# Expert tiles of 256 rows, weights as the stationary operand, brought by DMA into one of two stages

## The chip, the cores and the metric

The kernel runs on one core of a Trainium2 chip. The metric is the device time of one execution in microseconds. The core has five engines with queues of their own: PE (matmul, with PEld for its weight loads), DVE, ACT, POOL and SP, which here issues plain DMAs; POOL issues the indirect ones.

## The reference, cut to what matters

One transformer layer on 4 x 1024 tokens of width 128: a gated linear attention over the sequence, then a mixture of experts. The change touches the routed part of the second:

```python
shared = sum(_ffn(xf, sw1[i], sw2[i], sw3[i]) for i in range(2))      # two experts for all tokens
logits = xf @ router_w.T + expert_bias
rw, sel = jax.lax.top_k(logits, 2)                                     # two of eight experts a token
rw = softmax(rw)
out = sum over the 8 experts of combine[:, e] * _ffn(xf, w1[e], w2[e], w3[e])
_ffn(x, w1, w2, w3) = silu(x @ w1.T) * (x @ w3.T) @ w2.T               # 128 -> 256 -> 128
```

## The kernel before

All engines run hand-written programs with semaphores. First come eight blocks of 512 tokens: the attention of block i beside the shared experts and the routing of block i-1. For every token and each of its two experts, POOL writes the normalised row (129 words: 128 values and, last, the row's number in `y_dram`) with an indirect DMA into that expert's region of `h_dram`. When all blocks are through, `table_of_tiles` on DVE makes, from the counts per expert, two tables: `tile_row`, the first row of each tile in `h_dram`, and `tile_expert`, its expert. A region's last tile is filled up with rows of `pads`, and the number of tiles is fixed (NTILE): 72 tiles of 128 rows, whatever the counts.

Then the tile stage, in TURNS turns of U = 12 tiles. Tile j passes through:

- SP loads `tile_row[j]` into a register and issues the DMA of 128 rows into `rows[:, u]`, one of U places (u is the tile's number in the turn). It waits before that for `s_yrow[u]`, the scatter of the tile that had the place before.
- PE, `rows_T`: transposes the rows into a bank `at`. ACT (`hi`) and DVE (`lo`) split them into two float32r halves in `t_hi` and `t_lo`.
- PE, `first`: three matmuls of 512 columns with the rows' halves as the stationary operand and the expert's `w13_hi` and `w13_lo` (all experts lie in SBUF) as the moving one. Their address comes from a register; the registers of a turn are loaded together at its head.
- ACT (`silu_rows`), DVE (`gated`): G = silu(first half) * second half, with the rows as partitions.
- PE, `G_T`: two transposes of G, and DVE (`take_GT`) copies them to SBUF.
- PE, `second`: two f32 matmuls with `w_2`, into `ybank` or `obank`. ACT (`take_y`) copies y into `y_sb[:, u]`.
- POOL: a one-column product (`carrier`) and the indirect DMA that scatters the 128 rows of y into `y_dram` and counts `s_yrow[u]`.

In step u of a turn PE runs first(u), rows_T(u + AHEAD), G_T(u - BEHIND_T), second(u - BEHIND_D), with AHEAD, BEHIND_T, BEHIND_D = 2, 2, 3; the other engines' queues have orders that match. After the last scatter has landed, SP loads y from `y_dram`, ACT, DVE and POOL combine both experts' rows with the weights and the residual, and SP stores the output.

`S`, the state of the attention, is free in the tile stage; `rows`, `y_sb` and `t_silu` lie in it.

Of the kernel before, what the change touches and what calls it, by code (L numbers as in the profile page):

```python
# [78 lines left out]
U = 12  # L79
RING = 4  # L80
AHEAD, BEHIND_T, BEHIND_D = 2, 2, 3


def build(nc, x, cmod, attw, wg12, w13T, w2T, bias, consts, ids, tiles, pads, H, out):
# [11 lines left out]
    REG = NTOK + P  # L96
# [4 lines left out]
    assert NTILE % U == 0 and U % RING == 0 and NTILE >= 2 * NTOK // P + NEXP - 1 and TURNS >= 3  # L101

    h_dram = nc.dram_tensor("h_dram", [NEXP * REG + (NTILE - 2 * NTOK // P) * P, ROW], F32).ap()
    y_dram = nc.dram_tensor("y_dram", [2 * NTOK + pads.shape[0] * P, P], F32).ap()
# [5 lines left out]
    with ExitStack() as ctx:  # L110
# [7 lines left out]
        def parts(whole, *widths):  # L118
# [127 lines left out]
        tile_expert = sb("tile_expert", [1, NTILE + BEHIND_D], I32)  # L246


        rows, y_sb, t_silu = (a.rearrange("p (u n) -> p u n", n=n) for a, n in zip(
            parts(S[:, :, :].rearrange("p v n -> p (v n)"), U * ROW, U * P, 2 * HID), (ROW, P, HID)))  # L250
        t_G = upd[:, 0:2, :].rearrange("p a (r n) -> p (a r) n", n=HID)
        t_GT = qS[:, :, :].rearrange("p a (r n) -> p (a r) n", n=HID)
        t_hi, t_lo = (a[:, :].rearrange("p (r n) -> p r n", n=P) for a in (vT_hi, vT_lo))
# [95 lines left out]
        s_trow = [sem(f"s_trow{u}") for u in range(U)]  # L349
        s_yrow = [sem(f"s_yrow{u}") for u in range(U)]  # L350
# [6 lines left out]
        s_tGt = sem("s_tGt")  # L357
        s_tGT = sem("s_tGT")
# [51 lines left out]
        def _(sp):  # L410
# [14 lines left out]
            sp.dma_start(h_dram[NEXP * REG:, :].rearrange("(n p) w -> n p w", p=P),  # L425
# [3 lines left out]
            for e in range(NEXP):  # L429
                r = sp.value_load(pad_row[0:1, e:e + 1], min_val=e * REG, max_val=e * REG + NTOK)  # L430
                sp.dma_start(h_dram[bass.ds(r, P), :], pads[e, :, :]).then_inc(s_pad, 16)
# [11 lines left out]
            for u in range(U):  # L443
                sp.wait_ge(s_yrow[u], 16 * TURNS)
# [14 lines left out]
        def _(pe):  # L459
# [279 lines left out]
            w_hi = w13_hi[:, NSH:, :].rearrange("p e n -> p (e n)")  # L739
            w_lo = w13_lo[:, NSH:, :].rearrange("p e n -> p (e n)")  # L740
            w_2 = w2_sb[:, NSH:, :, :].rearrange("p e c n -> p (e c n)")
            experts = []

            def rows_T(q, u):
                j = q * U + u
                wait(pe, s_trow[u], 16 * q + 16)
                wait(pe, s_thi, j - 1)
                wait(pe, s_tlo, j - 1)
                pe.transpose(at[u % 2][:, 0:P], rows[:, u, 0:P], ident[:, :]).then_inc(s_tr, 1)  # L749

            def first(q, u):
                j = q * U + u
                e = experts[BEHIND_D + u]
                wait(pe, s_thi, j + 1)
                wait(pe, s_tlo, j + 1)
                wait(pe, s_tG, j - 1)
                w = bass.ds(e * 2 * HID, 2 * HID)
                pe.matmul(ff[u % 2][:, :], t_lo[:, u % RING, :], w_hi[:, w], start=True, stop=False)  # L758
                pe.matmul(ff[u % 2][:, :], t_hi[:, u % RING, :], w_hi[:, w], start=False, stop=False)  # L759
                pe.matmul(ff[u % 2][:, :], t_hi[:, u % RING, :], w_lo[:, w], start=False, stop=True).then_inc(s_tf1, 1)  # L760

            def G_T(q, u):
                j = q * U + u
                wait(pe, s_tG, j + 1)
                wait(pe, s_tGT, j - 1)
                for c in range(NC):
                    ins = pe.transpose(ff[2 + u % 2][:, c * P:(c + 1) * P], t_G[:, u % RING, c * P:(c + 1) * P], ident[:, :])  # L767
                ins.then_inc(s_tGt, 1)

            def second(q, u, column=None):  # L770
                j = q * U + u
                e = experts[BEHIND_D + u - (0 if column is None else column)]
                bank = (ybank, obank)[u % 2]
                wait(pe, s_tGT, j + 1)
                wait(pe, s_ty, j - 1)
                for c in range(NC):
                    ins = pe.matmul(bank[:, 0:P], t_GT[:, u % RING, c * P:(c + 1) * P],  # L777
                                    w_2[:, bass.ds(e * HID + c * P, P)], start=(c == 0), stop=(c == NC - 1))
                ins.then_inc(s_tf2, 1)

            def body(q, start, end):
                experts[:] = nc.values_load_multi_w_load_instructions(
                    tile_expert[0:1, bass.ds(q * U, U + BEHIND_D)], engines=(mybir.EngineType.PE,), min_val=0,
                    max_val=NEXP - 1, skip_runtime_bounds_check_because="the table holds minima with NEXP - 1")[1]
                for u in range(U):
                    first(q, u)
                    step(rows_T, q, u, AHEAD, start, end)
                    step(G_T, q, u, -BEHIND_T, start, end)
                    step(lambda q, s: second(q, s, U if s > u else 0), q, u, -BEHIND_D, start, end)
                if end:  # L790
                    for n in range(BEHIND_D):
                        if n >= BEHIND_D - BEHIND_T:
                            G_T(q, U - BEHIND_D + n)
                        second(q, U - BEHIND_D + n)
# [6 lines left out]
        def _(act):  # L801
# [136 lines left out]
            def hi(q, u):  # L938
                j = q * U + u
                wait(act, s_tr, j + 1)  # L940
                wait(act, s_tf1, j - RING + 1)
                act.activation(t_hi[:, u % RING, :], at[u % 2][:, 0:P], ACT.Copy).then_inc(s_thi, 1)

            def silu_rows(q, u):
                j = q * U + u
                wait(act, s_tf1, j + 1)
                wait(act, s_tG, j - 1)
                act.activation(t_silu[:, u % 2, :], ff[u % 2][:, 0:HID], ACT.Silu).then_inc(s_tsilu, 1)  # L948

            def take_y(q, u):  # L950
                j = q * U + u
                wait(act, s_tf2, j + 1)
                wait(act, s_yrow[u], 16 * q)
                act.activation(y_sb[:, u, :], (ybank, obank)[u % 2][:, 0:P], ACT.Copy).then_inc(s_ty, 1)

            def body(q, start, end):
                for u in range(U):
                    silu_rows(q, u)
                    step(hi, q, u, AHEAD, start, end)
                    step(take_y, q, u, -BEHIND_D, start, end)  # L960
                if end:
                    for n in range(BEHIND_D):
                        take_y(q, U - BEHIND_D + n)
# [15 lines left out]
        def _(pool):  # L979
# [82 lines left out]
            def body(q, start, end):  # L1062
                for u in range(U):
# [4 lines left out]
                    wait(pool, s_trow[u], 16 * q + 16)  # L1068
                    pool.tensor_tensor(carrier[:, 3:4], keep[:, 0:1], keep[:, 0:1], ALU.mult).then_inc(s_tcar, 1)  # L1069
                    pool.indirect_dma_start(  # L1070
                        out=y_dram[:, :], out_offset=bass.IndirectOffsetOnAxis(ap=rows[:, u, P:P + 1].bitcast(I32), axis=0),
                        in_=y_sb[:, u, :], in_offset=None).then_inc(s_yrow[u], 16)
# [10 lines left out]
        def _(dve):  # L1083
# [49 lines left out]
            dve.memset(earlier[:, NT, :], 0.0)  # L1133
            link(dve.memset(tile_expert[:, :], 0))
# [23 lines left out]
            def table_of_tiles():  # L1158
# [6 lines left out]
                link(dve.tensor_scalar(ntiles_i[:, :], counts[:, :], float(P - 1), None, ALU.add))  # L1165
# [385 lines left out]
```

## Time and profile before

| | us |
|---|---|
| median of 3 runs | 600.07 (599.37 to 605.8) |
| span of the profiled execution | 570.4 |
| busy in it: PE, DVE, POOL, ACT | 426.7, 431.5, 349.2, 203.0 |

The span is from the first to the last instruction of one profiled execution; the device time of a run has something more around it. In the rows, a line such as L440 is a line of the kernel before; a name before `<-` is what is written and the names behind it are read, by the buffer that lies there (`S` for `rows` and `y_sb`, `qS` for `t_GT`, `vT_hi` for `t_hi`, `upd` for `t_G`). PE records an f32 matmul as more than one pass. "SPq" and "PEldq" are the sequencers of SP and PE, "issue" is time in which the engine waited for nothing that the profile shows.

### The profile page before, as it was taken

What the parts mean: (1) busy time and instruction counts of PE and PEld (TensorE: products, weight loads), DVE (VectorE), ACT (ScalarE), POOL (GpSimd) and SP (SyncE); (2) the same over time, 40 slices, a digit from 0 to 9 for tenths busy, and PEclk for the clock granted to TensorE, in tenths of its full rate; (3) what the DMA queues carried; (4) which work ended last, traced back from release to release, by engine and by line L of the source; (5) the groups of instructions that cost most, each with busy time, mean ns of one, the idle gap of its engine ahead of it and who ended that gap; (6) DMA issues with size and microseconds to landing.
All of it is one profiled execution on the core that took longest, in us unless ns stands there. A gap on an engine that the chain in (4) does not pass through costs nothing.

```text
span 570.4 us, 9158 instructions
## 1 busy us (share of the span) xinstructions
PE 426.7 (75%) x2018; PEld 305.1 (53%) x2019; DVE 431.5 (76%) x1112; ACT 203.0 (36%) x507; POOL 349.2 (61%) x350
## 2 busy tenths in 40 slices
PE   4745867976978777887888789794789899899300
PEld 4522644653654554554564375483567787788200
DVE  4899899799799689789889879945445565566285
ACT  3650351451351252252253241121145455455170
POOL 0245666586676667577568558564447776777553
PEclk9977669989879889889898895996889999999855
DMA  9600000000000000000000010010222322232293
GB/s 266 269 1 0 0 1 0 25 15 0 25 14 0 19 19 0 7 30 0 5 32 0 0 37 0 1 39 0 80 66 81 94 79 78 79 88 71 85 298 92
DMA packets 32955, 28.44 MB, mean 50 GB/s; under 512 B 4362, under 2 KB 29970, under 8 KB 32658
## 3 DMA queue, kind: packets, MB, share of 16 engines
q1 hardware_dynamic: 28578, 19.20, 12.0%
q0 software_dynamic: 4352, 8.95, 4.7%
q8 instruction: 9, 0.15, 0.1%
q14 instruction: 16, 0.13, 0.1%
HBM read 17.10 MB, written 12.10 MB: 51 GB/s over the span
## 4 chain that ended last, share of the span: by engine, by line
DVE 36%; PE 34%; issue 15%; POOL 8%; DMA 2%; ACT 2%; SPq 1%; DVEq 1%; POOLq 1%; ACTq 0%
DVE S L1296 7%; POOL qS L1011 5%; PE ff L758 3%; PE obank L599 3%; PE ff L759 3%; PE ff L760 3%; PE obank L777 3%; PE ff L767 3%; PE ybank L777 2%; DVE upd L1288 2%; DVE S L1451 2%; PE at L614 2%; PE at L749 1%; DVE work L1204 1%; PE ff L462 1%
## 5 line engine op out<-in xcount | busy, mean ns | idle before, releaser
L1011 POOL TENSOR_TENSOR qS<-S,qT 128x512 f32<-128x512 f32 x56 | 90.9, 1631 | 54.4 <-DVE S L1296 49.7
L1296 DVE TENSOR_TENSOR_SCAN S<-decay,S,upd 128x512 f32<-128x512 f32 x64 | 93.0, 1463 | 0.0
L599 PE MATMUL obank<-qS,gather_v 128*128 128x512 f32 x112 | 67.9, 693 | 29.9 <-POOL qS L1011 29.1
L1070 POOL DMA_INDIRECT y_dram<-S x72 | 70.9, 984 | 15.7 <-POOL carrier L1069 8.6
L1039 POOL DMA_INDIRECT h_dram<-h,target_i x64 | 62.2, 973 | 21.1 <-issue 20.1
L1431 DVE COPY qS<-ff 128x256 f32<-128x256 f32 x72 | 30.6, 424 | 46.4 <-PE ff L767 45.3
L875 ACT ACTIVATE work<-ff 128x512 f32<-128x512 f32 x32 | 19.1, 597 | 110.3 <-PE ff L464 110.3
L586 PE MATMUL at<-vT_hi,spread_v 128*128 128x512 f32 x64 | 34.8, 544 | 28.1 <-DVE upd L1288 12.6
L599 PEld LDWEIGHTS obank<-qS,gather_v 128*128 128x128 f32 x112 | 20.6, 206 | 53.3 <-POOL qS L1011 47.2
L462 PE MATMUL ff<-h2T_hi,w_hi 128*128 128x512 f32 x64 | 39.6, 619 | 7.4 <-POOL h2T_lo L1019 3.7
L1288 DVE TENSOR_TENSOR upd<-at,khat 128x512 f32<-128x512 f32 x64 | 43.3, 676 | 2.4 <-DVE khat L1281 1.1
L948 ACT ACTIVATE S<-ff 128x256 f32<-128x256 f32 x72 | 27.6, 383 | 41.4 <-PE ff L760 41.4
L758 PE MATMUL ff<-w_hi,vT_lo 128*128 x72 | 35.3, 490 | 8.3 <-DVE vT_lo L1417 6.5
L586 PEld LDWEIGHTS at<-vT_hi,spread_v 128*128 128x128 f32 x64 | 13.8, 216 | 46.3 <-DVE upd L1288 25.9
L1204 DVE TENSOR_TENSOR work<-ff,work 128x512 f32<-128x512 f32 x32 | 21.5, 675 | 22.1 <-ACT work L875 21.9
L1424 DVE TENSOR_TENSOR upd<-ff,S 128x256 f32<-128x256 f32 x72 | 29.9, 415 | 3.4 <-ACT S L948 3.4
L653 PE MATMUL ybank<-w_sb,work 128*128 128x128 f32 x256 | 30.0, 275 | 1.5 <-DVE work L1204 1.5
L653 PEld LDWEIGHTS ybank<-w_sb,work 128*128 128x128 f32 x256 | 29.6, 192 | 2.5 <-DVE work L1204 2.0
L587 PE MATMUL at<-vT_lo,spread_v 128*128 128x512 f32 x64 | 29.8, 465 | 0.0
L759 PE MATMUL ff<-w_hi,vT_hi 128*128 x72 | 29.0, 402 | 0.0
L760 PE MATMUL ff<-w_lo,vT_hi 128*128 x72 | 28.8, 400 | 0.0
L463 PE MATMUL ff<-h2T_lo,w_hi 128*128 128x512 f32 x64 | 28.1, 439 | 0.0
(209 smaller groups left out, 1086.7 us busy)
## 6 DMA issues: line engine op xcount, KB each, us to landing
S<-h_dram SPq DMA_DIRECT2D x72, 64.5 KB, 1.8
work<-in_w13T SPq DMA_DIRECT2D x1, 2560.0 KB, 10.3
xall<-in_x SPq DMA_DIRECT2D x8, 256.0 KB, 5.4
w_hi<-y_dram SPq DMA_DIRECT2D x8, 256.0 KB, 5.4
w_lo<-y_dram SPq DMA_DIRECT2D x8, 256.0 KB, 5.3
out<-work SPq DMA_DIRECT2D x8, 256.0 KB, 2.5
w_sb<-in_w2T SPq DMA_DIRECT2D x1, 1280.0 KB, 13.0
y_dram<-S POOLq DMA_INDIRECT x72, 2.3
```

What stands on the lines that cost most here:

```text
L462: pe.matmul(dst, w_hi, h_hi, start=True, stop=False)
L586: pe.matmul(bank[:, :], spread_v[:, v, :], vT_hi[:, :], start=True, stop=False)
L599: pe.matmul(obank[:, :], gather_v[:, v, :], product, start=(v == 0), stop=(v == HD - 1)) \
L653: ins = pe.matmul(ybank[:, t * P:(t + 1) * P], G[:, NC * e + c, t * P:(t + 1) * P], w2_sb[:, e, c, :], start=(n == 0), stop=(n == len(term ...
L758: pe.matmul(ff[u % 2][:, :], t_lo[:, u % RING, :], w_hi[:, w], start=True, stop=False)
L759: pe.matmul(ff[u % 2][:, :], t_hi[:, u % RING, :], w_hi[:, w], start=False, stop=False)
L760: pe.matmul(ff[u % 2][:, :], t_hi[:, u % RING, :], w_lo[:, w], start=False, stop=True).then_inc(s_tf1, 1)
L1011: pool.tensor_tensor(qS[:, v % 2, :], S[:, v, :], qT[:, :], ALU.mult).then_inc(s_qS, 1)
L1039: pool.indirect_dma_start(out=h_dram[:, :], out_offset=bass.IndirectOffsetOnAxis(ap=target_i[:, k, t:t + 1], axis=0), in_=h2[:, k, t, :], ...
L1070: pool.indirect_dma_start(out=y_dram[:, :], out_offset=bass.IndirectOffsetOnAxis(ap=rows[:, u, P:P + 1].bitcast(I32), axis=0), in_=y_sb[:, ...
L1288: dve.tensor_tensor(upd[:, v % 3, :], at[v % 2][:, :], khat[:, :], ALU.mult).then_inc(s_upd, 1)
L1296: dve.tensor_tensor_scan(S[:, v, :], decay[:, :], upd[:, v % 3, :], S0[:, v:v + 1], ALU.mult, ALU.add) \
```

## The change

Tiles have 256 rows (TR = SUB * P), and there are 40 of them in 5 turns of U = 8. `rows` and `y_sb` have RING = 4 places, each with two blocks of 128 rows, and a place is used twice in a turn (LAPS = U // RING). In `first` the weights are the stationary operand and the rows' halves the moving one, so that G comes out with its 256 hidden values as partitions; `G_T` and `take_GT` go. The stationary operand is addressed without a register: SP copies the expert's 2 x 256 KB of weights per tile, from `w13_hi` and `w13_lo` in SBUF, into one of two stages (`hT_hi`, `h2T_hi` and `hT_lo`, `h2T_lo`, which are free by then). `second` follows one step behind `first`, and loads its own expert's number on PE. POOL issues two scatters for each tile. The diff, without the changed shapes, the pads' and the tables' sizes:

```diff
-U = 12
+SUB = 2
+TR = SUB * P
+U = 8
 RING = 4
-AHEAD, BEHIND_T, BEHIND_D = 2, 2, 3
+PAIR = 2
+AHEAD, BEHIND = 2, 1
...
+            sp.wait_ge(s_f1, NF1 * NB)
             sp.wait_ge(s_scatter, 16 * 2 * NT * NB)
             def body(q, first, last):
                 for u in range(U):
-                    r = sp.value_load(tile_row[0:1, bass.ds(q * U + u, 1)], min_val=0, max_val=h_dram.shape[0] - P)
-                    wait(sp, s_yrow[u], 16 * q)
-                    sp.dma_start(rows[:, u, :], h_dram[bass.ds(r, P), :]).then_inc(s_trow[u], 16)
+                    r = sp.value_load(tile_row[0:1, bass.ds(q * U + u, 1)], min_val=0, max_val=h_dram.shape[0] - TR)
+                    wait(sp, s_yrow[u % RING], 16 * SUB * (LAPS * q + u // RING))
+                    sp.dma_start(rows[:, u % RING, :, :], h_dram[bass.ds(r, TR), :].rearrange("(s p) w -> p s w", p=P)) \
+                        .then_inc(s_trow[u % RING], 16)
+                    e = sp.value_load(tile_expert[0:1, bass.ds(q * U + u, 1)], min_val=0, max_val=NEXP - 1)
+                    wait(sp, s_tf1, 2 * (q * U + u - 1))
+                    for whole, stage in ((w13_hi, st_hi), (w13_lo, st_lo)):
+                        sp.dma_start(stage[u % PAIR][:, :].bitcast(F32),
+                                     whole[:, NSH:, :].rearrange("p e n -> p (e n)")[:, bass.ds(e * 2 * HID, 2 * HID)].bitcast(F32)) \
+                            .then_inc(s_stage[u % PAIR], 16)
...
             def rows_T(q, u):
                 j = q * U + u
-                wait(pe, s_trow[u], 16 * q + 16)
+                wait(pe, s_trow[u % RING], 16 * (LAPS * q + u // RING) + 16)
                 wait(pe, s_thi, j - 1)
                 wait(pe, s_tlo, j - 1)
-                pe.transpose(at[u % 2][:, 0:P], rows[:, u, 0:P], ident[:, :]).then_inc(s_tr, 1)
+                for k in range(SUB):
+                    ins = pe.transpose(at[u % 2][:, k * P:(k + 1) * P], rows[:, u % RING, k, 0:P], ident[:, :])
+                ins.then_inc(s_tr, 1)
             def first(q, u):
                 j = q * U + u
-                e = experts[BEHIND_D + u]
+                wait(pe, s_stage[u % PAIR], 32 * (U // PAIR * q + u // PAIR + 1))
                 wait(pe, s_thi, j + 1)
                 wait(pe, s_tlo, j + 1)
                 wait(pe, s_tG, j - 1)
-                w = bass.ds(e * 2 * HID, 2 * HID)
-                pe.matmul(ff[u % 2][:, :], t_lo[:, u % RING, :], w_hi[:, w], start=True, stop=False)
-                pe.matmul(ff[u % 2][:, :], t_hi[:, u % RING, :], w_hi[:, w], start=False, stop=False)
-                pe.matmul(ff[u % 2][:, :], t_hi[:, u % RING, :], w_lo[:, w], start=False, stop=True).then_inc(s_tf1, 1)
-            def G_T(q, u):
+                hi, lo = t_hi[:, u % PAIR, :], t_lo[:, u % PAIR, :]
+                for k in range(2):
+                    for c in range(NC):
+                        dst = ff[2 * (u % 2) + k][:, c * TR:(c + 1) * TR]
+                        w = slice(k * HID + c * P, k * HID + (c + 1) * P)
+                        pe.matmul(dst, st_hi[u % PAIR][:, w], hi, start=True, stop=False)
+                        pe.matmul(dst, st_hi[u % PAIR][:, w], lo, start=False, stop=False)
+                        ins = pe.matmul(dst, st_lo[u % PAIR][:, w], hi, start=False, stop=True)
+                    ins.then_inc(s_tf1, 1)
+            def second(q, u):
                 j = q * U + u
+                e = nc.values_load_multi_w_load_instructions(
+                    tile_expert[0:1, bass.ds(j, 1)], engines=(mybir.EngineType.PE,), min_val=0, max_val=NEXP - 1,
+                    skip_runtime_bounds_check_because="the table holds minima with NEXP - 1")[1][0]
+                bank = (ybank, obank)[u % 2]
                 wait(pe, s_tG, j + 1)
...
                 wait(pe, s_ty, j - 1)
-                for c in range(NC):
-                    ins = pe.matmul(bank[:, 0:P], t_GT[:, u % RING, c * P:(c + 1) * P],
-                                    w_2[:, bass.ds(e * HID + c * P, P)], start=(c == 0), stop=(c == NC - 1))
+                for k in range(SUB):
+                    for c in range(NC):
+                        ins = pe.matmul(bank[:, k * P:(k + 1) * P], t_G[:, u % PAIR, c * TR + k * P:c * TR + (k + 1) * P],
+                                        w_2[:, bass.ds(e * HID + c * P, P)], start=(c == 0), stop=(c == NC - 1))
                 ins.then_inc(s_tf2, 1)
...
                 for u in range(U):
                     first(q, u)
                     step(rows_T, q, u, AHEAD, start, end)
-                    step(G_T, q, u, -BEHIND_T, start, end)
-                    step(lambda q, s: second(q, s, U if s > u else 0), q, u, -BEHIND_D, start, end)
+                    step(second, q, u, -BEHIND, start, end)
...
             def take_y(q, u):
                 j = q * U + u
                 wait(act, s_tf2, j + 1)
-                wait(act, s_yrow[u], 16 * q)
-                act.activation(y_sb[:, u, :], (ybank, obank)[u % 2][:, 0:P], ACT.Copy).then_inc(s_ty, 1)
+                wait(act, s_yrow[u % RING], 16 * SUB * (LAPS * q + u // RING))
+                act.activation(y_sb[:, u % RING, :, :].rearrange("p s n -> p (s n)"), (ybank, obank)[u % 2][:, 0:TR], ACT.Copy) \
+                    .then_inc(s_ty, 1)
...
-                    wait(pool, s_trow[u], 16 * q + 16)
+                    wait(pool, s_trow[u % RING], 16 * (LAPS * q + u // RING) + 16)
                     pool.tensor_tensor(carrier[:, 3:4], keep[:, 0:1], keep[:, 0:1], ALU.mult).then_inc(s_tcar, 1)
...
+                    for k in range(SUB):
+                        pool.indirect_dma_start(
+                            out=y_dram[:, :],
+                            out_offset=bass.IndirectOffsetOnAxis(ap=rows[:, u % RING, k, P:P + 1].bitcast(I32), axis=0),
+                            in_=y_sb[:, u % RING, k, :], in_offset=None).then_inc(s_yrow[u % RING], 16)
```

In this diff `hi`, `silu_rows` and `gated` take 256 rows (256, 512 and 512 columns), and `second` and `take_y` run one step behind `first`.

## Rows read from the trace of the kernel before

**Rows 1.** Busy time by stretches: us (instructions) per engine, then clock, DMA share, GB/s.
```profile
core 0: us, PE busy (x) PEld busy (x) DVE busy (x) ACT busy (x) POOL busy (x), PEclk, DMA share, GB/s
414.00:538.00 124.00, 110.56 (x720) 94.94 (x720) 68.94 (x216) 60.06 (x216) 87.35 (x146) 0.98 0.27 76
...
453.00:472.00 19.00, 17.54 (x119) 15.19 (x118) 11.43 (x36) 9.68 (x36) 13.81 (x24) 1.00 0.30 83
```

**Rows 2.** Order of time, PE in one tile: start, length, engine, line, operation.
```profile
462.29 0.48 PE L758 MATMUL ff<-w_hi,vT_lo 128*128 x1
...
463.07 0.27 PE L749 MATMUL at<-consts_sb,S 128*128 128x128 f32 x1
...
463.17 0.38 PE L767 MATMUL ff<-consts_sb,upd 128*128 128x128 f32 x2
...
463.39 0.61 PE L777 MATMUL ybank<-w_sb,qS 128*128 x4
...
463.76 0.48 PE L758 MATMUL ff<-w_hi,vT_lo 128*128 x1
```

**Rows 3.** Groups by line and shape: busy us, mean ns, idle before, releasers.
```profile
L1070 POOL DMA_INDIRECT y_dram<-S x72 | 70.9, 984 | 15.7 <-POOL carrier L1069 8.6 <-issue 6.9
...
L1431 DVE COPY qS<-ff 128x256 f32<-128x256 f32 x72 | 30.6, 424 | 46.4 <-PE ff L767 45.3 <-issue 1.0
...
L948 ACT ACTIVATE S<-ff 128x256 f32<-128x256 f32 x72 | 27.6, 383 | 41.4 <-PE ff L760 41.4
```

**Rows 4.** Waits of SP's queue: us in total, times, longest.
```profile
SPq L440 <- DMA y_dram<-S: 24.0, 40, 2.1
```

**Rows 5.** Order of time, from the copy of y to its scatter.
```profile
456.76 0.28 ACT L954 ACTIVATE S<-obank 128x128 f32<-128x128 f32 x1 [0.23 <-PE obank L777]
...
457.13 0.18 POOL L1069 TENSOR_TENSOR carrier<-consts_sb 128x1 f32<-128x1 f32 x1 [1.95 <-ACT S L954]
...
457.47 0.98 POOL L1070 DMA_INDIRECT y_dram<-S  x1 [0.16 <-POOL carrier L1069]
```

**Rows 6.** Order of time, end of the tile stage.
```profile
532.04 0.71 PE L777 MATMUL ybank<-w_sb,qS 128*128 x4 [0.61 <-DVE qS L1431]
...
532.78 0.28 ACT L954 ACTIVATE S<-ybank 128x128 f32<-128x128 f32 x1 [1.26 <-PE ybank L777]
...
535.57 0.98 POOL L1070 DMA_INDIRECT y_dram<-S  x1 [0.16 <-issue]
537.91 0.40 SPq L448 DMA_DIRECT2D w_hi<-y_dram  x1
```

**Rows 7.** Order of time, two indirect DMAs of POOL in a row.
```profile
402.10 0.96 POOL L1039 DMA_INDIRECT h_dram<-h,target_i  x1 [0.30 <-issue]
...
403.37 0.95 POOL L1039 DMA_INDIRECT h_dram<-h,target_i  x1 [0.30 <-issue]
```

**Rows 8.** DMA issues: queue, operation, count, KB each, us from issue to landing.
```profile
S<-h_dram SPq DMA_DIRECT2D x72, 64.5 KB, 1.8
...
out<-work SPq DMA_DIRECT2D x8, 256.0 KB, 2.5
```

**Rows 9.** Register loads (ns min/median/max, first and last start), and SP's first issues.
```profile
L438 SPq TENSOR_LOAD <-tile_row x72: 263/276/381, 410.2 to 520.2; - x72
...
L782 PEldq TENSOR_LOAD <-tile_expert x6: 1573/1598/1767, 414.3 to 510.7; - x6
...
411.39 12.90 SPq L440 DMA_DIRECT2D S<-h_dram  x12
```

**Rows 10.** Stretches and order of time where PE stands and starts again.
```profile
400.00:403.30 3.30, 1.11 (x5) 0.59 (x3) 2.94 (x7) 0.69 (x2) 2.45 (x3) 0.97 0.38 101
403.30:407.00 3.70, 3.65 (x9) 2.86 (x10) 0.70 (x2) 0.60 (x1) 2.88 (x3) 0.54 0.39 107
...
404.19 0.63 PE L464 MATMUL ff<-h2T_hi,w_lo 128*128 128x512 f32 x1
...
404.62 0.63 PE L462 MATMUL ff<-h2T_hi,w_hi 128*128 128x512 f32 x1
```

More of the change, by code:

```diff
@@ L95, in build @@
     NTOK = B * N
-    REG = NTOK + P
+    REG = NTOK + TR
     NTILE = tiles.shape[1] - NEXP
@@ L100, in build @@
     assert D == P and NC == 2 and NEXP == 8 and NSH == 2 and HD == 8 and N % TB == 0
-    assert NTILE % U == 0 and U % RING == 0 and NTILE >= 2 * NTOK // P + NEXP - 1 and TURNS >= 3
-    h_dram = nc.dram_tensor("h_dram", [NEXP * REG + (NTILE - 2 * NTOK // P) * P, ROW], F32).ap()
-    y_dram = nc.dram_tensor("y_dram", [2 * NTOK + pads.shape[0] * P, P], F32).ap()
+    LAPS = U // RING
+    assert NTILE % U == 0 and U % RING == 0 and NTILE >= 2 * NTOK // TR + NEXP - 1 and TURNS >= 3
+    h_dram = nc.dram_tensor("h_dram", [NEXP * REG + (NTILE - 2 * NTOK // TR) * TR, ROW], F32).ap()
+    y_dram = nc.dram_tensor("y_dram", [2 * NTOK + pads.shape[0] * TR, P], F32).ap()
     y_tiles = y_dram[0:2 * NTOK].rearrange("(n p) d -> p n d", p=P)
@@ L245, in build @@
         tile_row = sb("tile_row", [1, NTILE], I32)
[L246 to L253, printed above, removed]
+        tile_expert = sb("tile_expert", [1, NTILE], I32)
+        rows, y_sb, t_silu = parts(S[:, :, :].rearrange("p v n -> p (v n)"), RING * SUB * ROW, RING * SUB * P, PAIR * NC * TR)
+        rows = rows.rearrange("p (u s w) -> p u s w", s=SUB, w=ROW)
+        y_sb = y_sb.rearrange("p (u s n) -> p u s n", s=SUB, n=P)
+        t_silu = t_silu.rearrange("p (u n) -> p u n", n=NC * TR)
+        t_G = upd[:, 0:PAIR, :]
+        st_hi, st_lo = (hT_hi, h2T_hi), (hT_lo, h2T_lo)
+        t_hi, t_lo = (a[:, :].rearrange("p (r n) -> p r n", n=TR) for a in (vT_hi, vT_lo))
         y_in = [a[:, 0:NB, :].bitcast(F32) for a in (w13_hi, w13_lo)]
@@ L348, in build @@
         s_pad = sem("s_pad")
-        s_trow = [sem(f"s_trow{u}") for u in range(U)]
-        s_yrow = [sem(f"s_yrow{u}") for u in range(U)]
+        s_trow = [sem(f"s_trow{u}") for u in range(RING)]
+        s_stage = [sem(f"s_stage{u}") for u in range(PAIR)]
+        s_yrow = [sem(f"s_yrow{u}") for u in range(RING)]
         s_tr = sem("s_tr")
@@ L787, in body @@
                     step(rows_T, q, u, AHEAD, start, end)
-                    step(G_T, q, u, -BEHIND_T, start, end)
-                    step(lambda q, s: second(q, s, U if s > u else 0), q, u, -BEHIND_D, start, end)
+                    step(second, q, u, -BEHIND, start, end)
                 if end:
[L791 to L794, printed above, removed]
+                    second(q, U - BEHIND)
             for u in range(AHEAD):
@@ L959, in body @@
                     step(hi, q, u, AHEAD, start, end)
-                    step(take_y, q, u, -BEHIND_D, start, end)
+                    step(take_y, q, u, -BEHIND, start, end)
                 if end:
-                    for n in range(BEHIND_D):
-                        take_y(q, U - BEHIND_D + n)
+                    take_y(q, U - BEHIND)
             for u in range(AHEAD):
@@ L1415, in lo @@
                 wait(dve, s_thi, j + 1)
-                wait(dve, s_tf1, j - RING + 1)
-                dve.tensor_tensor(t_lo[:, u % RING, :], at[u % 2][:, 0:P], t_hi[:, u % RING, :].bitcast(F32), ALU.subtract) \
+                wait(dve, s_tf1, 2 * (j - 1))
+                dve.tensor_tensor(t_lo[:, u % PAIR, :], at[u % 2][:, 0:TR], t_hi[:, u % PAIR, :].bitcast(F32), ALU.subtract) \
                     .then_inc(s_tlo, 1)
@@ L1422, in gated @@
                 wait(dve, s_tsilu, j + 1)
-                wait(dve, s_tGt, j - RING + 1)
-                dve.tensor_tensor(t_G[:, u % RING, :], ff[u % 2][:, HID:2 * HID], t_silu[:, u % 2, :], ALU.mult) \
+                wait(dve, s_tf1, 2 * j + 2)
+                wait(dve, s_tf2, j - 1)
+                dve.tensor_tensor(t_G[:, u % PAIR, :], ff[2 * (u % 2) + 1][:, :], t_silu[:, u % PAIR, :], ALU.mult) \
                     .then_inc(s_tG, 1)
-            def take_GT(q, u):
-                j = q * U + u
-                wait(dve, s_tGt, j + 1)
-                wait(dve, s_tf2, j - RING + 1)
-                dve.tensor_copy(t_GT[:, u % RING, :], ff[2 + u % 2][:, 0:HID]).then_inc(s_tGT, 1)
             def body(q, start, end):
                 for u in range(U):
-                    step(take_GT, q, u, -BEHIND_T, start, end)
                     gated(q, u)
                     step(lo, q, u, AHEAD, start, end)
-                if end:
-                    for n in range(BEHIND_T):
-                        take_GT(q, U - BEHIND_T + n)
             for u in range(AHEAD):
@@ L1486, in constants @@
         np.broadcast_to(np.arange(NB) % BPB != 0, (P, NB)),
-        np.broadcast_to(np.arange(NEXP) * (NB * TB + P), (P, NEXP)),
+        np.broadcast_to(np.arange(NEXP) * (NB * TB + TR), (P, NEXP)),
     ]
```

55 lines of the change are left out of this document (17 added, 38 removed).

## The prediction

> **What bounds the kernel now.** I read the page's span first, then the busy time by stretches, then the order of time inside one tile, then the waits of SP's queue and the DMA issues. The change touches only the routed experts' tiles, and in the busy time by stretches these run from 414 to 538 us, 124 of the 570.4 us of the profiled execution [rows 1]. In their middle PE is busy 17.54 of 19 us at the full clock (1.00, the level of 2.4 GHz), DVE 11.4, ACT 9.7, POOL 13.8, and the DMA engines move 83 GB/s at a share of 0.30. PE sets the pace. One tile of 128 rows shows how: the first of its three 512-column matmuls starts at 462.29 and that of the next tile at 463.76, so a tile is 1.47 us. The three take 0.78 (462.29 to 463.07), the rows' transpose 0.10, the two transposes of G 0.22, the second product, two f32 matmuls in four passes, the rest [rows 2]. A pass of 128 f32 columns is thus 0.11 us. POOL is close behind: one scatter of y takes 0.98 us, 72 of them 70.9 [rows 3].
>
> SP is not felt. It waits 24.0 us in 40 pieces on landed scatters, none over 2.1 us [rows 4], because the ring of `rows` and `y_sb` has 12 places: the rows of tile j wait for the scatter of tile j-12, whose second product PE ran in step j-9 (three behind), while the rows are transposed in step j-2. Seven steps of 1.47 us, 10.3 us, lie between the two. This distance is the number to carry into the change.
>
> **The change: the work on the engines.** 72 tiles of 128 rows become 40 of 256. On PE a tile has 12 matmuls of 256 columns, 3072 columns as two old tiles had, so about 2 x 0.78 = 1.5 us or less, two row transposes (0.2) and the second product in eight passes (0.9); the transposes of G go. That is 2.5 us against 2 x 1.47 = 2.94, and 40 x 2.5 = 100 us against 72 x 1.47 = 106: minus 6 us if PE still set the pace. DVE loses the copy of the transposed G, 30.6 us in all [rows 3], which was beside PE's work and is worth nothing by itself. POOL gets 80 scatters instead of 72, and one carrier for two scatters: 0.18 + 0.16 + 0.98 + 0.29 + 0.98 + 0.15 = 2.74 us a tile [rows 5, 7], 110 us in all, hidden only while another loop is longer.
>
> **The change: the weights' copies.** Each tile adds two DMAs of 256 KB from SBUF to SBUF, for which the trace has no row. The nearest with an SBUF source is the store of the output, 256 KB, 2.5 us to landing [rows 8]; a second one behind it adds 0.4 of issue and some 0.4 of transfer, so 3.3 us for the pair; with a far slower rate, a quarter of this, 13. They are issued behind the rows of the same tile, after one more register load (0.28 us and its register instructions) [rows 9], and are wanted by `first` two steps later. With the step that comes out below, over 8 us, even 13 us are covered. What they cost is nothing, as long as they do not stretch other landings.
>
> **The change: the ring of four.** This is the step that decides. `rows` and `y_sb` now have RING = 4 places, so SP's issue of the rows of tile j waits until both scatters of tile j-4 have landed. PE's order in a step u is first(u), rows_T(u+2), second(u-1). So second(j-4) is the last thing in step j-3, and rows_T(j) stands in step j-2, behind first(j-2) alone and ahead of second(j-3). Not seven steps but part of one lies between them, and everything from the end of second(j-4) to the transpose of tile j is a chain that repeats once per tile. Queued behind the waiting rows issue on SP are the weights of tile j and the rows of j+1; queued behind the waiting transpose on PE are second(j-3) and first(j-1). One turn of the loop, with PE at 1.2 GHz (why is said below):
>
> - second product, from its start to the start of ACT's copy: 0.74 us with four passes at the full clock (532.04 to 532.78) [rows 6]; with eight passes 0.74 + 4 x 0.11 = 1.17; at half the clock 8 x 0.21 and a tail of 0.4: 2.1
> - ACT's copy of 256 columns: 0.38, as L948 has [rows 3]
> - to the carrier, carrier, to the scatter: 0.09 + 0.18 + 0.16 = 0.43 [rows 5]
> - the first scatter until the second starts: 1.27 [rows 7]
> - the second scatter's start until SP issues the next transfer: 2.34 (535.57 to 537.91) [rows 6]
> - rows to landing: 1.8 for 64.5 KB [rows 8]; the second 64.5 KB at 83 GB/s for a share of 0.30, that is 277 GB/s [rows 1], add 0.23: 2.03
> - PE's wakening 0.1, two transposes at half the clock 0.43
> - PE's register load in `second` (one load is 0.28 on SP, fifteen at once 1.6 on PE) [rows 9]: 0.5 with its register instructions, partly under the transposes: 0.2
>
> The sum is 2.1 + 0.38 + 0.43 + 1.27 + 2.34 + 2.03 + 0.1 + 0.43 + 0.2 = 9.28, say 9.3 us a tile. first(j-2), 2.6 us at half the clock, runs meanwhile beside the scatters (4.4 us) and costs nothing; DVE's and ACT's work for the neighbouring tiles (under 2 us of each) does neither.
>
> The page "DMA: Bandwidth & Descriptors" of the Trainium skill (section on the anatomy of one DMA) says that a DMA has a fixed cost of about 2.0 us, most of it the wait for the last write's receipt, and a part that goes with bytes at 436 GB/s. By that estimate the rows would take 2.3 us and not 2.03, and the sum would be 9.6 us, 10 us more over the stage. By the same rule doubling the tile hardly lengthens a landing, but a ring so short that each step holds two of them pays two fixed costs at every tile, and that speaks against this change.
>
> **The clock.** In a loop of 9.3 us PE works 2.1 + 2.6 + 0.4, some 5 us, in one burst and then stands for 4. The rows show what less than that does: from 400 to 403.3 PE is busy 1.11 of 3.3 us, and in the next 3.7 us, with PE full, the granted clock is 0.54 and 512 columns take 0.43 us (404.19 to 404.62) [rows 10]; the full level is back only after that. So transposes and second product, which open the burst, run at 1.2 GHz. At the full clock the loop would be 1.17 + 0.38 + 0.43 + 1.27 + 2.34 + 2.03 + 0.1 + 0.2 + 0.4 = 8.3 us.
>
> **The sum.** The wait holds for tiles 4 to 39: 36 turns. Before them: SP issued one load and one transfer each 1.1 us (12 in 12.9) [rows 9]; with two loads and three DMAs 2.75 us a tile, rows 0 go out at 411.5, weights 0 from 412.6, rows 1 at 414.1, weights 1 at 415.2, rows 2 at 416.7. The weights of tile 2 wait for first(0), which ends about 419.4, and rows 3 stand behind them: issued 421.0, landed 423.1. second(0) follows, and ACT takes y(0) at about 426. Then 36 x 9.3 = 335: 761. Then two steps with no wait and the last three tiles' scatters, at 2.74 us a tile and 2.3 to land: about 14, so the last lands at 775 us against 538 now. Plus 237 us. Everything before 411 and the 32.5 us behind the last landing stay. The span goes from 570.4 to 807, and with the 29.7 us by which the median of the runs (600.07) is above the profiled span, the time is 837 us.
>
> **Rivals.**
>
> 1. PE keeps the full clock: 8.3 us a turn, 36 x 1.0 = 36 us less, 801 us. For it: a burst of 5 us may bring the clock back in its later part. Against: the part on the loop is the burst's beginning, right after 4 us of standing.
> 2. The copies stretch the loop: they share the engines with the rows and the scatters. If SBUF to SBUF moved at a quarter of the store's rate, 13 us a pair, the rows of the next tile would stand behind them: p about 13 + 0.8 + a part of the rows' landing, 14 us, and 36 x 5 more: some 1000 us. At slight contention, 10.5 us a turn: 880.
> 3. The ring does not bind, the staging does: weights j wait for first(j-2). Issue to landing 3.3, rows j+1 behind it 0.5, transposes 0.2, load 0.2, second 0.9, first 1.3, wake 0.1: 6.5 us per two tiles, 3.3 a tile, 132 us, with 14 at both ends 146 against 124: 622 us. This needs the scatter to have landed long before, for which nothing speaks.
> 4. Not slower: the loop closes in less than POOL's 2.74 us a tile, by an order of PE or SP other than I read; POOL then sets the pace, 9 + 110 + 2.3 = 121 us against 124, 597 us. It decides from the point where both scatters, their landing and the rows' landing, 1.27 + 2.34 + 2.03 = 5.6 us, fit between the two points in PE's order at 2.74 us a tile; that takes two or three more places than the ring has.
>
> **How the numbers follow.** The forecast with PE cold has 0.62, full clock 0.18, stretched landings 0.14, staging 0.03, POOL's pace 0.03. A microsecond in the turn is 36 in the time. The range of the forecast itself is 8.9 to 9.9 us a turn, 822 to 859; with the full clock and slight contention it is 790 to 880, which leaves out rivals 3 and 4 and the heavy half of 2. About 1% is what a measurement can tell from no change: faster 0.01, same 0.03, slower 0.96.
>
> **What would show it.** Right: in the waits of SP, the rows' issue waiting for y_dram's landing 36 times, 4 us or more each; first matmuls of neighbouring tiles some 9.3 us apart; a granted clock near 0.5 to 0.7 in the stage; POOL mostly idle; PE idle before the row transposes, not before `first`. Wrong: PE idle before `first` on the weights' landing (rival 3); a spacing near 2.7 (rival 4); landing of the rows far over 2 us (rival 2); passes 0.11 us apart in the second product (rival 1).

## The result and the profile after

The changed kernel takes 856.16 us (median, 853.55 to 864.48) against 602.93 us for the kernel before in the same comparison: 1.42 times, with a 95% interval of 1.411 to 1.428. The forecast was 837 us in a range of 790 to 880. The profiled execution of the changed kernel has a span of 862.7 us and is the longest of its runs (864.48).

The waits come first, those of SP's queue and two of PE and POOL in the stage (engine line waited for, us in total, times, longest). L446 is the issue of the rows, L451 that of the weights, L760 the row transposes.

```profile
SPq L446 <- DMA y_dram<-S: 231.9, 36, 7.4
...
SPq L451 <- PE ff L776: 1.1, 1, 1.1
```

```profile
POOL carrier L1074 <- ACT S L959: 191.4, 25, 17.3
PE at L760 <- DMA S<-h_dram: 182.7, 40, 7.0
```

Where SP waited 24.0 us in 40 pieces of at most 2.1 [rows 4], it now waits 231.9 us in 36, one for each tile from the fifth on and 6.4 us in the mean. Its wait for `first`, which guards the weights' stages, is 1.1 us in all. PE stands before the row transposes, not before `first`.

Busy time by stretch, from SP's first rows issue to the first load of y behind the last landing (columns as in [rows 1]):

```profile
440.50:828.70 388.20, 194.96 (x880) 171.00 (x880) 44.67 (x80) 54.55 (x120) 85.23 (x120) 0.66 0.24 82
```

The stage lasts 388.2 us; in the trace of before it lasts 126.5 by the same two marks (411.39 to 537.91) [rows 6, 9]. PE is busy half of it, at a mean clock of 0.66, and POOL 22%. The DMA issues show no slow transfer:

```profile
S<-h_dram SPq DMA_DIRECT2D x40, 129.0 KB, 2.2
hT_hi<-w_hi SPq DMA_DIRECT2D x20, 256.0 KB, 2.3
hT_lo<-w_lo SPq DMA_DIRECT2D x20, 256.0 KB, 2.4
...
y_dram<-S POOLq DMA_INDIRECT x80, 2.2
```

One turn of the loop in the order of time, late in the stage (start, length, engine, line, operation):

```profile
799.88 0.39 SPq L446 DMA_DIRECT2D S<-h_dram  x1
...
802.07 0.69 PE L760 MATMUL at<-consts_sb,S 128*128 128x128 f32 x2 [4.62 <-DMA S<-h_dram]
...
802.92 2.07 PE L789 MATMUL obank<-w_sb,upd 128*128 x8 [0.16 <-issue]
...
805.03 0.38 ACT L959 ACTIVATE S<-obank 128x256 f32<-128x256 f32 x1 [1.85 <-PE obank L789]
...
805.55 0.19 POOL L1074 TENSOR_TENSOR carrier<-consts_sb 128x1 f32<-128x1 f32 x1 [7.10 <-issue]
...
806.19 0.98 POOL L1076 DMA_INDIRECT y_dram<-S  x1 [0.46 <-issue]
...
807.48 0.96 POOL L1076 DMA_INDIRECT y_dram<-S  x1 [0.30 <-issue]
...
809.87 0.39 SPq L446 DMA_DIRECT2D S<-h_dram  x1
...
813.01 2.07 PE L789 MATMUL ybank<-w_sb,upd 128*128 x8 [0.15 <-issue]
```

Read it as a circle: rows of tile j issued (799.88), landed and transposed (802.07), second product of tile j-3 behind them (802.92), its copy, the carrier, two scatters, and at 809.87 SP may issue the rows of tile j+1, since the scatters of j-3 have landed. From one second product to the next are 10.09 us. Over the 35 turns from the rows of tile 4 (460.51) to those of tile 39 (809.87) the mean is 9.98.

### The profile page after: what moved, and what is told of

It reads as the page before. It is cut to its first block and busy times, and to the rows that moved or that the text cites. A ratio compares the mean times of both kernels' runs of the same rounds, so it can differ in the third digit from the quotient of the medians.

```text
span 862.7 us, 8695 instructions
## 1 busy us (share of the span) xinstructions
PE 520.2 (60%) x2178; PEld 387.9 (45%) x2179; DVE 396.9 (46%) x975; ACT 197.9 (23%) x411; POOL 343.2 (40%) x326
## 5 line engine op out<-in xcount | busy, mean ns | idle before, releaser
L760 PE MATMUL at<-consts_sb,S 128*128 128x128 f32 x80 | 27.0, 439 | 182.7 <-DMA S<-h_dram 182.7
L1423 DVE TENSOR_TENSOR vT_lo<-at,vT_hi 128x256 fp32r<-128x256 f32 x40 | 17.0, 425 | 205.8 <-ACT vT_hi L947 205.8
L760 PEld LDWEIGHTS at<-consts_sb,S 128*128 128x128 f32 x80 | 11.4, 201 | 192.1 <-DMA S<-h_dram 168.7
L1431 DVE TENSOR_TENSOR upd<-ff,S 128x512 f32<-128x512 f32 x40 | 27.7, 692 | 138.4 <-PE ff L776 138.4
L947 ACT ACTIVATE vT_hi<-at 128x256 fp32r<-128x256 f32 x40 | 15.3, 383 | 226.5 <-PE at L760 226.5
L789 PE MATMUL obank<-w_sb,upd 128*128 x160 | 39.6, 425 | 4.6 <-issue 4.2
L789 PE MATMUL ybank<-w_sb,upd 128*128 x160 | 39.5, 425 | 4.0 <-issue 3.9
L789 PEld LDWEIGHTS obank<-w_sb,upd 128*128 128x128 f32 x160 | 34.2, 316 | 11.9 <-issue 11.9
L666 PEld LDWEIGHTS ybank<-w_sb,work 128*128 128x128 f32 x256 | 37.9, 234 | 3.8 <-issue 2.8
L789 PEld LDWEIGHTS ybank<-w_sb,upd 128*128 128x128 f32 x160 | 34.0, 314 | 11.3 <-issue 11.3
```

What stands on the lines that cost most here:

```text
L666: ins = pe.matmul(ybank[:, t * P:(t + 1) * P], G[:, NC * e + c, t * P:(t + 1) * P], w2_sb[:, e, c, :], start=(n == 0), stop=(n == len(term ...
L760: ins = pe.transpose(at[u % 2][:, k * P:(k + 1) * P], rows[:, u % RING, k, 0:P], ident[:, :])
L789: ins = pe.matmul(bank[:, k * P:(k + 1) * P], t_G[:, u % PAIR, c * TR + k * P:c * TR + (k + 1) * P], w_2[:, bass.ds(e * HID + c * P, P)], ...
L1431: dve.tensor_tensor(t_G[:, u % PAIR, :], ff[2 * (u % 2) + 1][:, :], t_silu[:, u % PAIR, :], ALU.mult) \
```

## The experiments

In two of the comparisons the kernel before takes 603 and 605 us, in the three others 573 to 574. So the experiments are compared by two lengths from their traces as well: the stage (first rows issue to first load of y; 126.5 before, 388.2 after) and the spacing of the rows issues of tiles 4 to 39 (9.98 after).

### Where the 28 us lie

The kernel before again:

> The kernel before, profiled a second time. The profiled span of before that the prediction used (570.4 us) is 30 us under its timed runs, while that of the changed kernel is 2 us under its own. If the missing 28 us are work outside the tile stage that differs from execution to execution, this span is near 598 us, with the tile stage again 124 to 127 us and the rest in the eight blocks. If they are launch time outside the span, the span is near 570 again.

It took 574.58 us, with a span of 572.7.

```profile
400.72 9.54 SPq L431 DMA_DIRECT2D h_dram<-in_pads  x8
413.33 4.77 SPq L440 DMA_DIRECT2D S<-h_dram  x5
```

```profile
540.00 0.40 SPq L448 DMA_DIRECT2D w_hi<-y_dram  x1
```

Neither of the two readings held. The time is 1.9 us above the span, so the missing 28 us are not launch time; but the whole execution was the short one again. The changed kernel gave the better clue:

> The changed kernel itself, on the chip of the other experiments, where the kernel before takes 573 to 574 us, 28 less than in the comparison of the result. If those 28 us lie in the blocks and the change's cost in the tile stage alone, this takes 573 + 257 = 830 us, with about 9.9 us a tile. If the stage scales with the rest, 1.42 times 573, 814 us.

It took 855.39 us beside a before of 605.45 (ratio 1.41), so the comparison fell among the long ones and the forecast of 830 was for the others. Its trace starts the stage at 432.15 and keeps 388.9 us for it (9.97 a tile), while the variants of the changed kernel that ran beside a before of 573 or 574, whose eight blocks are the same code, start it at 411 to 414. So some 20 to 28 us come and go ahead of the stage, and the stage's length does not move. They are not in one place. Between the first scatters of neighbouring blocks, from the second block to the seventh, the trace with small copies has 43.6 to 45.6 us, that of the result 49.5 to 51.2 in four of the five distances, and this one 45.4 to 49.5. The issue of the eight pads right ahead of the stage shows it too, here with eight places (beside a before of 573) and in the result:

```profile
401.50 9.55 SPq L438 DMA_DIRECT2D h_dram<-in_pads  x8
```

```profile
423.95 13.55 SPq L436 DMA_DIRECT2D h_dram<-in_pads  x8
```

The kernel before, profiled a third time:

> The kernel before, profiled a third time, to see where the 30 us lie that separate its timed runs of about 603 us from those of about 573. The changed kernel's own traces begin the tile stage at 432 and 441 us where it took 855 to 864, and its variants' at 411 to 414 beside a before of 573. If this execution takes about 600 us, its tile stage should begin at 438 to 446 us and last 126 us as in the first trace; if about 573, this adds nothing but a repeat.

It took 573.91 us, stage from 412.15 to 538.72: a repeat, and no trace of before in a 600 us execution exists. Why the blocks take longer stays open.

### Five places instead of four

```diff
-U = 8
-RING = 4
+U = 10
+RING = 5
```

> The changed kernel with five places in rows and y_sb and turns of ten tiles (U = 10, RING = 5), nothing else. If the ring of places sets the pace, one loop of 10.0 us (8.9 with PE at the full clock) now covers two tiles: 4.5 to 5.0 us a tile, about 180 us less, 665 to 685 us. If the weights' copies or their waits set it, nothing changes: 850 to 860 us.

664.89 us. The stage is 214.3 us, the spacing 5.17 us a tile, about half of 9.98, as one loop now carries two tiles. That is a little over the 4.5 to 5.0 expected. The 665 to 685 us had been worked out from 856, that is from a before of 603 and not 573, so the stage is what can be held against them: it is 174 us shorter, where about 180 had been expected. The waits of SP's queue:

```profile
SPq L451 <- PE ff L776: 38.3, 18, 3.8
SPq L446 <- DMA y_dram<-S: 24.2, 20, 3.3
```

One more place takes 174 us out of the stage. The wait for the scatters falls from 231.9 to 24.2 us, and the next one comes up, that of the weights for `first`.

### Eight places

```diff
-RING = 4
+RING = 8
...
-        rows, y_sb, t_silu = parts(S[...], RING * SUB * ROW, RING * SUB * P, PAIR * NC * TR)
+        rows = S[...][:, 0:RING * SUB * ROW]
+        y_sb = work[:, 0:RING * SUB * P]
+        t_silu = qS[...]
```

> The changed kernel with eight places (y_sb moved to work, t_silu to qS to make room). If the ring was the bound, it is gone: what is left is POOL's 2.74 us a tile or the weights' chain of 3.3 us a tile (issue to landing 3.3, rows behind it, transposes, second, first: 6.5 us per two tiles), so a tile stage of 124 to 150 us and 595 to 630 us in all. If the copies take bandwidth from everything, it stays over 700 us.

641.44 us beside 573.42 for before (1.118, 1.116 to 1.121); stage 190.7 us, 4.51 us a tile. SP no longer waits for a scatter in the loop, so the ring is gone as a bound. But the price of the weights' chain was too low: 3.3 us a tile was expected and 4.5 measured, and a stage of 124 to 150 us was missed. The order of time shows where (L453 weights, L448 rows, L762 transposes, L791 second product, L776 to L778 `first`):

```profile
504.74 0.41 PE L778 MATMUL ff<-vT_hi,hT_lo 128*128 128x256 f32 x1
...
505.30 0.51 SPq L453 DMA_DIRECT2D hT_hi<-w_hi  x1
...
505.92 0.53 SPq L453 DMA_DIRECT2D hT_lo<-w_lo  x1
...
507.58 0.39 SPq L448 DMA_DIRECT2D S<-h_dram  x1
...
509.85 0.20 PEld L762 LDWEIGHTS at<-consts_sb,S 128*128 128x128 f32 x2 [2.10 <-DMA S<-h_dram]
...
510.86 1.15 PE L791 MATMUL ybank<-w_sb,upd 128*128 x8 [0.57 <-issue]
...
511.77 0.36 PE L776 MATMUL ff<-vT_hi,hT_hi 128*128 128x256 f32 x1
...
513.58 0.51 SPq L453 DMA_DIRECT2D hT_hi<-w_hi  x1
```

The rows of tile j+1 stand in SP's queue behind the weights of tile j, which wait for first(j-2). They go out 2.28 us after the first weights' DMA (two issues and a register load) and start PE 2.27 us later; PE stands for them with second and first behind. From one copy into this stage to the next, two tiles on, are 8.28 us, where the rival's sum had 6.5: 4.55 until the rows are there and not 3.8, 1.01 for transposes and register load and not 0.4, 2.72 for second, first and SP's release and not 2.3. In other turns PE's clock is low as well, and the mean of two tiles is 9.0.

### Small copies

Only the weights' bytes are cut; the weights of the later tiles are left out, so this kernel doesn't compute the layer.

```diff
+                    n = 2 * HID if first and u < PAIR else 16
...
-                        sp.dma_start(stage[u % PAIR][:, :]..., whole[...][:, bass.ds(e * 2 * HID, 2 * HID)]...)
+                        sp.dma_start(stage[u % PAIR][:, 0:n]..., whole[...][:, bass.ds(e * 2 * HID, n)]...)
```

> The changed kernel with the copies of the weights cut from 512 to 16 columns per partition from the third tile on (the weights of later tiles are left out, so those products are made with the wrong ones); the same number of DMAs, waits and register loads. If the ring sets the pace and the copies are covered: within 2% of 856 us, at most some 0.2 us a tile less (7 us). If their transfer stretches landings or sets the pace: 36 times the stretch less, under 800 us.

With four places: 828.46 us beside a before of 573.42; stage 378.9 us, 9.75 us a tile. The two expected times start from 856, that is from a before of 603, so the stages decide. SP still waits 233.4 us in 36 pieces for the scatters. The bytes of the weights, 97% of which are gone, cost 0.23 us a tile, some 9 us of 388, a little more than the 0.2 and 7 allowed. But for this they lie beside the loop, as the prediction put them.

> Eight places and the copies cut to 16 columns from the third tile on (later tiles' weights are left out). Beside the run with eight places and full copies this gives what the bytes cost once the ring is gone: if the weights' chain sets the pace there, its landing falls from 3.3 to about 2.4 us, 0.4 us a tile, some 15 us less; if POOL sets it, the same time within 1%.

With eight places: 624.28 us beside 574.09 (1.087, 1.081 to 1.094), stage 179.3 us against 190.7, 4.20 a tile against 4.51. There the bytes give 11 us of the stage (17 between the two times), where some 15 had been expected, and the rest of the chain, queueing and landing times that hardly depend on size, stays.

### A third scatter

```diff
-                    for k in range(SUB):
+                    for k, target in ((0, y_dram), (1, y_dram), (1, z_dram)):
                         pool.indirect_dma_start(
-                            out=y_dram[:, :],
+                            out=target[:, :],
```

> The changed kernel with a third scatter per tile, into a tensor that nobody reads. If scatter, landing and rows form the loop of each tile, its 1.29 us are added 36 times: 46 us more, about 902 us. POOL is busy only some 25% of the time in the stage, so if the loop goes by another way nothing changes: 856 us.

886.73 us beside a before of 574.09. Its stage is 439.4 us against 388.2, and the spacing 11.25 us against 9.98: 1.27 us a tile more, one scatter's distance. The 902 us had been built on the long executions; by the stage the forecast of 46 us was met (51, with the tiles at both ends). SP waits for the new tensor's scatter:

```profile
SPq L447 <- DMA z_dram<-S: 278.9, 36, 8.7
```

POOL was idle 78% of the stage, yet 1.27 us of its time cost 1.27 us each: it is on the loop.

### Keeping PE busy

```diff
                     first(q, u)
+                    for _ in range(30):
+                        pe.matmul(at[u % 2][:, TR:2 * TR], spread_v[:, 0, :],
+                                  spread_v[:, 0:2, :].rearrange("p v n -> p (v n)"), start=True, stop=True)
```

> The changed kernel with 30 matmuls of 256 columns after each first, written to an unused part of the bank and used by nobody; they fill most of PE's standing time before the row transposes. If the low clock is a part of the loop through the second product and the transposes (2.11 to 1.2 us, 0.4 to 0.2), the turn falls by 1.0 to 1.2 us to some 8.9: 815 to 825 us. If PE's speed isn't on the loop: no change, or slower, as the extra matmuls get in the way.

834.71 us beside a before of 574.09; stage 386.5 us against 388.2, 9.65 us a tile. The 0.33 us a tile hardly show in the stage, since the extra matmuls lengthen both its ends: from the rows of tile 3 to those of tile 4 by 3.5 us, from the last rows to its end by 6.2. A turn of some 8.9 us had been expected, 1.0 to 1.2 less. In the mean that was missed, and in single turns it was met:

```profile
602.77 0.39 SPq L447 DMA_DIRECT2D S<-h_dram  x1
...
606.02 1.15 PE L790 MATMUL ybank<-w_sb,upd 128*128 x8 [0.51 <-issue]
...
607.21 0.39 ACT L963 ACTIVATE S<-ybank 128x256 f32<-128x256 f32 x1 [1.20 <-PE ybank L790]
...
611.71 0.38 SPq L447 DMA_DIRECT2D S<-h_dram  x1
```

```profile
608.40:612.20 3.80, 3.79 (x32) 3.58 (x30) 0.69 (x1) 0.12 (x1) 1.56 (x2) 1.00 0.11 35
...
626.00:631.50 5.50, 5.50 (x40) 5.50 (x40) 0.69 (x1) 0.98 (x2) 2.13 (x3) 0.79 0.08 24
```

In this turn the clock is 1.00, the second product comes to ACT in 1.19 us and not 2.11, and the turn is 8.94 us. In others the clock falls (0.79 with PE full). Of the 36 turns, counted from one second product to the next, nine have ACT's copy after at most 1.2 us and take 8.87 us in the mean (8.55 to 9.33); sixteen have it after 2.0 or more and take 10.1 (9.8 to 11.1). So the low clock costs some 1.1 to 1.2 us of a turn where it is low, and this way of keeping it up gets back 0.33 of that in the mean. What lets it fall isn't settled. PE still waits before the transposes, but the length of that wait alone doesn't decide. In two turns one behind the other it was 2.08 and 2.07 us, and the second product ran at the full level in the first and at half in the second:

```profile
488.60 0.44 PE L761 MATMUL at<-consts_sb,S 128*128 128x128 f32 x2 [2.08 <-DMA S<-h_dram]
489.18 1.15 PE L790 MATMUL ybank<-w_sb,upd 128*128 x8
...
497.41 0.44 PE L761 MATMUL at<-consts_sb,S 128*128 128x128 f32 x2 [2.07 <-DMA S<-h_dram]
498.51 2.06 PE L790 MATMUL obank<-w_sb,upd 128*128 x8 [0.66 <-issue]
```

### The ring alone, in the kernel before

```diff
+PLACES = 6
...
-                    wait(sp, s_yrow[u], 16 * q)
-                    sp.dma_start(rows[:, u, :], ...)
+                    wait(sp, s_yrow[u % PLACES], 16 * (LAPS * q + u // PLACES))
+                    sp.dma_start(rows[:, u % PLACES, :], ...)
```

> The kernel before, with tiles of 128 rows, its own products and no copies of weights, but six places in rows and y_sb instead of twelve. Its second product runs three steps behind, so that six places leave one step between second(j-6) and the transpose of tile j, as four do in the changed kernel. If the ring alone makes the loss: 6.3 (full clock) to 7.4 us (half) a tile, 66 times, 905 to 975 us. If the larger tiles or the copies are needed for it: within 5% of 600 us.

929.96 us beside a before of 574.09 (1.62). Nothing of the change is in it but a shorter ring.

```profile
SPq L442 <- DMA y_dram<-S: 385.3, 66, 7.7
```

```profile
602.69 0.47 PE L751 MATMUL at<-consts_sb,S 128*128 128x128 f32 x1 [3.71 <-DMA S<-h_dram]
...
609.57 0.47 PE L751 MATMUL at<-consts_sb,S 128*128 128x128 f32 x1 [3.84 <-DMA S<-h_dram]
```

6.88 us from one tile to the next, and 6.96 in the mean of the 66 turns, where it had been 1.47 [rows 2]: inside the 6.3 to 7.4 worked out from the rows. The distance between two points in PE's order is enough for the whole loss.

### The rows issued ahead of the weights

SP issues the rows three tiles ahead of the weights, with eight places:

```diff
+                    step(load_rows, q, u, LEAD, first, last)     # LEAD = 3: rows of tile u + 3
                     e = sp.value_load(tile_expert[0:1, bass.ds(q * U + u, 1)], ...)
                     wait(sp, s_tf1, 2 * (q * U + u - 1))
                     for whole, stage in ((w13_hi, st_hi), (w13_lo, st_lo)): ...
```

> Eight places, and SP issues the rows three tiles ahead of the weights (rows j+3, then weights j), so that no rows stand behind the wait of the weights. The run with eight places alone took 4.7 us a tile, its rows issue standing behind the weights' wait for first(j-2). If that queueing is its bound, this falls to the next one, POOL's 2.8 or PE's 2.5 and a register load a tile: 3.0 to 3.3 us, 575 to 600 us. If the weights' landing itself is the bound, it stays near 640.

632.74 us beside 605.45 for before (1.045, 1.036 to 1.053); stage 171.3 us against 190.7. The queueing was worth 19 us of the stage, 0.5 a tile of the 1.2 that the chain's price had been too low by. The 575 to 600 us were worked out from a before of 573, so they can't be held against this time, but the 3.0 to 3.3 us a tile were not reached (3.9). What PE waits for now is mixed:

```profile
PE ff L782 <- DMA hT_lo<-w_lo: 22.6, 16, 4.7
...
PE ff L782 <- DMA h2T_lo<-w_lo: 10.3, 10, 1.8
```

These are the weights' landings, 33 us; the mean clock is 0.90, and PE is busy 119 of 171 us. With four matmuls more behind each `first`:

> As the run before with four matmuls of 256 columns, used by nobody, after each first. If PE's clock still falls in short waits there, they may give back up to 10 us; if PE is dense and at the full level already, they add 4 x 0.11 us a tile, up to 17 us.

634.62 us (1.051, 1.043 to 1.059), stage 169.2 us: no difference that can be told, neither the gain of up to 10 us nor the loss of up to 17. No version with staged weights beat the kernel before. The rest of its 45 us of stage was not taken apart.

## Why the prediction was right

- **The ring decides.** Right in place, number of waits (36) and order. Five places halve the spacing, eight remove the wait, and six places in the old kernel bring the loss back without anything else of the change.
- **The turn.** 9.28 us were predicted, 10.09 measured in the turn shown and 9.95 in the mean of the 36 turns from second(0) to second(36). By its terms:

| term | predicted | turn shown | mean of 36 |
|---|---|---|---|
| second product to ACT's copy | 2.1 | 2.11 | 2.11 |
| copy | 0.38 | 0.38 | 0.38 |
| to the carrier, carrier, to the scatter | 0.43 | 0.14 + 0.19 + 0.45 = 0.78 | 0.12 + 0.19 + 0.29 = 0.60 |
| first scatter to second | 1.27 | 1.29 | 1.31 |
| second scatter to SP's issue | 2.34 | 2.39 | 2.40 |
| rows to landing, PE's wakening | 2.13 | 2.29 | 2.24 |
| transposes and register load | 0.63 | 0.85 | 0.91 |

No term is far off, and all but two are too short. The largest miss in the mean is the last, 0.28, where the sum had put the register load at 0.2 behind the transposes. The carrier's is 0.17. Between the carrier's end and the first scatter there are 0.15 us in 19 turns, as in [rows 5], and 0.45 in 17, behind the same wait of POOL for some 7 us:

```profile
655.75 0.19 POOL L1074 TENSOR_TENSOR carrier<-consts_sb 128x1 f32<-128x1 f32 x1 [7.38 <-ACT S L959]
656.39 0.98 POOL L1076 DMA_INDIRECT y_dram<-S  x1 [0.46 <-issue]
...
666.03 0.19 POOL L1074 TENSOR_TENSOR carrier<-consts_sb 128x1 f32<-128x1 f32 x1 [7.40 <-ACT S L959]
666.38 0.99 POOL L1076 DMA_INDIRECT y_dram<-S  x1 [0.15 <-POOL carrier L1074]
```

So 0.7 us in all were missing, 25 us over 36 turns, which is the 25 by which the stage, 388.2 us, is longer than the 363.5 of the sum. The wakening of 0.1 has no row of its own; with a landing of 2.2 us of the 2.24 little is left for it.

- **PE's clock.** Right: second product and transposes run at half, and the turn at the full clock is 8.9 us as far as single turns of the experiment show it, where 8.3 had been forecast, 0.6 too short.
- **The copies are covered.** Right in the main: 2.3 to 2.4 us to landing, and a cost of 0.23 us a tile where none had been put down.
- **The landing by size.** The rows' 129 KB take 2.2 us to landing. The 2.3 us worked out by "DMA: Bandwidth & Descriptors" (the Trainium skill, section on the anatomy of one DMA) and the 2.03 from the rows enclose it. For the weights' copies the page's formula would give an estimate of 2.6 us for 256 KB and 2.0 for 8 KB; the traces have 2.3 to 2.4 and, in the run with small copies, 1.7. So most of a landing does not go with size, as the page says. Its formula is given for DMAs that GpSimd issues; for these, issued by SP, it comes out 0.1 to 0.3 us too high.
- **Start.** The stage starts 29 us later than in the sum (440.5 and not 411.5). None of it belongs to the change: SP's issue of the pads takes 13.55 us there and not 9.54, but the same eight DMAs take 9.53 to 9.56 in the variants that ran beside a before of 573 or 574, which start the stage at 411 to 414.
- **The 29.7 us** between median and span were a wrong reading that did little harm. They were carried over as a constant outside the span; the span is only 1.8 us short of the time in the same execution (862.7 and 864.48). The profiled execution of before was one with shorter blocks, and the changed one has the part ahead of the stage longer by 29 us, so both errors nearly cancel. For the profiled run: start +29, stage +25, tail +1.5, gap -28, together the 27 us from 837 to 864; its median is 8 us below it. With the shorter blocks the kernel would take an estimated 835 us (573 + 388 - 126.5), nearly the forecast, but by luck: 28 us too many outside the stage against 25 too few in it.
- **Rivals.** The full clock did not come by itself. The staging chain, rival 3, was priced at 3.3 us a tile; once the ring was out of the way it measured 4.5. The sum had left out part of SP's queue between the weights and the next rows, worth 0.5 of the 1.2, and had the steps on PE too short. The ratio of 1.42 leaves no room for POOL's pace.

## What to carry to other kernels

When a ring of buffers is shortened or a pipeline's depths are changed, count the steps, in the consumer's own order, between the instruction that frees a place and the one that needs its next content; that distance times the pace must cover release, transfer and landing, or the whole latency becomes the pace, whatever the engines' busy shares say. On a queue that executes in order, a transfer that must wait should not stand ahead of one that is free to go. And when a loop is priced by adding up small steps, expect the sum to be short: here every step but two was, by 0.04 to 0.28 us, and that made 25 us over 36 turns.

## What the runs showed of the hardware

- An indirect DMA on POOL started 0.15 or 0.45 us after the end of the instruction ahead of it, without a wait that the profile shows. Both stand in the changed kernel behind waits of some 7 us (0.15 at 666.38, 0.45 at 656.39) and in the dense stage of before (0.16 at 463.65, 0.45 at 462.27); what decides between them isn't known. Two indirect DMAs in a row started some 1.3 us apart (1.27 in [rows 7], 1.29 in the turn shown), with 0.95 to 1.0 us of POOL each.
- 256 KB copied within SBUF, 2 KB a partition, landed 2.3 to 2.4 us after issue in the changed kernel; with 64 bytes a partition it was 1.7.
- PE's granted clock was 0.79 over a stretch with PE full (5.50 of 5.50 us); the wait before that burst's transposes had been 1.21 us. From 489 to 496 it was 1.00, behind a wait of 2.08 us.
- The part ahead of the stage took 20 to 28 us more in some comparisons than in others with the same code, spread over the blocks and the issue of the pads (13.55 and 9.55 us); the cause isn't known.
